# One transformer layer with packed feed-forward weights: the first gate weights prepared one stage earlier, down pieces and row sums spread over other units

## The reference

```python
x = x + _layernorm(attention(_layernorm(x), Wq, Wkv, Wo, bo))
x = x + _layernorm(ffn(_layernorm(x), gate_Wq, up_Wq, down_Wq, scales, zeros))

# attention: 32 query heads of 32, 8 groups of keys and values, causal softmax
# ffn:
Wg, Wu, Wd = dequantize(gate), dequantize(up), dequantize(down)   # (w4 - zero) * scale, groups of 64
g = einsum('bsh,ih->bsi', x, Wg)
u = einsum('bsh,ih->bsi', x, Wu)
h = silu(g) * u
return einsum('bsi,hi->bsh', h, Wd)
```

## Time and profile before

| | us |
|---|---|
| median of 3 runs (2747.84 to 2748.58) | 2748.23 |
| profiled execution | 2746.93 |
| its span | 2745.1 |
| PE busy | 2628.1 |
| DVE busy | 1608.5 |
| POOL busy | 1164.5 |
| ACT busy | 953.3 |
| SP and ACT issue DMAs; moved in all | 209.93 MB |

### The profile page before, as it was taken

The page is one execution under the profiler, slowest core; times in us unless marked ns, Lnnn a source line. Parts: engine busy times, 40 slices in busy tenths (PEclk is TensorE's granted clock), DMA queues, the critical chain, the costliest instruction groups (busy, mean ns, idle before and its releaser), DMA issues. The chain is left out here.

```text
span 2745.1 us, 42051 instructions
## 1 busy us (share of the span) xinstructions
PE 2628.1 (96%) x17032; PEld 1113.8 (41%) x17032; DVE 1608.5 (59%) x1993; ACT 953.3 (35%) x1676; POOL 1164.5 (42%) x641
## 2 busy tenths in 40 slices
PE   6999899999999999999987999999999997999998
PEld 3445533333333333324443444444444443444443
DVE  6331778777787787825677688777777770101001
ACT  3111266666666666671112222332232220000000
POOL 0000177777777777771222334555555550100001
PEclk9999999999999999999998999999999998999999
DMA  4223101011010110003223322333333347332220
GB/s 172 81 77 97 31 17 30 17 46 30 17 30 17 43 33 17 2 1 128 94 76 106 94 74 92 107 111 101 113 109 105 106 143 264 113 120 72 72 72 31
DMA packets 180351, 209.93 MB, mean 76 GB/s; under 512 B 17620, under 2 KB 138708, under 8 KB 180180
## 3 DMA queue, kind: packets, MB, share of 16 engines
q1 hardware_dynamic: 175440, 198.11, 22.3%
q10 hardware_dynamic: 4740, 9.44, 0.9%
HBM read 146.28 MB, written 61.08 MB: 76 GB/s over the span
## 5 line engine op out<-in xcount | busy, mean ns | idle before, releaser
L788 POOL TENSOR_TENSOR c_prob<-c_prob 128x1024 f32<-128x1024 f32 (+1 forms) x285 | 600.2, 2125 | 517.7 <-ACT c_prob L651 515.3
L670 DVE TENSOR_REDUCE c_maxes<-c_s 128x2 f32<-128x1024 f32 (+3 forms) x640 | 645.6, 1058 | 198.8 <-PE c_s L500 198.8
L651 ACT ACTIVATE c_prob<-c_s 128x512 f32<-128x512 f32 (+1 forms) x1152 | 598.0, 571 | 300.3 <-PE c_s L522 185.0
L522 PE MATMUL c_s<-c_q,c_k 97*128 97x512 f16 (+3 forms) x1280 | 367.5, 353 | 10.1 <-ACT c_prob L651 1.7
L1346 PE MATMUL e_ps<-x_hi,e_w_hi 128*128 128x512 f16 x832 | 316.1, 380 | 15.4 <-DVE e_w_lo L1419 15.4
L1347 PE MATMUL e_ps<-x_lo,e_w_hi 128*128 128x512 f16 x832 | 316.0, 380 | 0.0
L1348 PE MATMUL e_ps<-x_hi,e_w_lo 128*128 128x512 f16 x832 | 315.9, 380 | 0.0
L537 PE MATMUL c_ctx<-c_prob,v_sb 128*32 128x512 f32 (+3 forms) x2560 | 293.7, 540 | 0.2 <-ACT c_c L635 0.2
L1731 POOL TENSOR_TENSOR e_w<-e_w,e_scales 128x1024 f32<-128x1024 f32 (+2 forms) x67 | 161.3, 2408 | 260.4 <-DVE e_w L1403 260.4
L522 PEld LDWEIGHTS c_s<-c_q,c_k 97*128 97x128 f16 x1280 | 111.4, 97 | 345.9 <-ACT c_prob L651 299.3
L77 DVE BATCH_NORM_STATS2 f_norm_stats<-f_yp 128x6 f32<-128x512 f32 x16 | 11.2, 699 | 409.0 <-PE f_yp L1884 409.0
(11 more groups left out here) (193 smaller groups left out, 3796.3 us busy)
## 6 DMA issues: line engine op xcount, KB each, us to landing
h_hi<-e_hh SPq DMA_DIRECT2D x84, 128.0 KB, 1.8
h_lo<-e_hl SPq DMA_DIRECT2D x84, 128.0 KB, 1.8
b_x<-L_attn_x SPq DMA_DIRECT2D x16, 512.0 KB, 6.3
c_q<-qk_hi SPq DMA_DIRECT2D x64, 128.0 KB, 3.1
d_x<-L_attn_x SPq DMA_DIRECT2D x16, 512.0 KB, 5.2
x_dram<-d_x SPq DMA_DIRECT2D x16, 512.0 KB, 2.6
f_x<-x_dram SPq DMA_DIRECT2D x8, 1024.0 KB, 7.0
out<-f_z SPq DMA_DIRECT2D x8, 1024.0 KB, 5.0
```

Of the source, the lines that this page charges most:

```text
L522: last = nc.tensor.matmul(S2[:, h % 2, at:at + w], K[:, g % 2, k * P:(k + 1) * P], Q[:, g % 2, b, h, q:q + w], start=True, stop=not diag)
L651: nc.scalar.activation(prob(g, s, 0, w)[:, h, :], S2[:, h % 2, 0:w], ACT.Exp, scale=exp_scale).then_inc(exp_done, 1)
L670: last = nc.vector.tensor_reduce(MAXES[:, g % 2, t // TPB, heads, t % TPB, u], S1[:, heads, at:at + w], AX.X, ALU.max)
L788: return nc.gpsimd.tensor_tensor(one, one, two, ALU.add)
```

## The change

Three things, and what they need:

- **First gate weights.** A new class `Opening` owns the buffers for preparing weights that `gate_and_up` made itself before. They lie in the memory of `c_hi` and `c_lo`, which now stay allocated to the end. In `project_context` SP loads the words, zeros and scales of the first two gate chunks once TensorE has read the context for the last time, ahead of the last `store_rows`. VectorE unpacks chunk 0 in the last pair's `body`, ahead of the second norm; GpSimd scales it after its last residual sum; ScalarE makes the high half ahead of the last `cut_turned`, VectorE the low half (`trail`) ahead of the same. `gate_and_up` starts with chunk 1.
- **Down pieces.** One piece in (q, 0) for all q except 5, the last included; two more in (1,1), one more in (2,1). The last unit (21,1) has none, (21,0) has one. Pieces from number 2 on are thereby made earlier: 2 and 3 in (1,1), 4 in (2,0), 5 in (2,1), 6 in (3,0), 7 in (4,0). In units of `made_beside` SP stores the piece ahead of the h of that unit.
- **Row sums.** Group (1,0) goes beside the remainder, unit (2,0); (1,1) and (1,2) are in (3,0), and (1,3) alone in (3,1).

In stage 4 the down weights of 16 chunks lie where the context was and those of the last chunk and the rest in a small buffer, so the last part is loaded by three DMAs for each half in place of two.

```diff
@@ -858,6 +861,10 @@
             with sp.Fori(0, PAIRS - 1) as i:
                 store_rows(i)
                 load_rows(i + 1)
+            sp.wait_ge(y_product, 2 * PAIRS)
+            for chunk in range(2):
+                opening.load(sp, chunk)
             store_rows(PAIRS - 1)
             for s in range(2):
                 sp.wait_ge(x1_stored[s], 16 * PAIRS)
@@ -922,6 +929,9 @@
                 if not last:
                     dve.wait_ge(x1_done, 2 * i + 1)
                     read_product(i + 1, 0)
+                else:
+                    dve.wait_ge(y_product, 2 * PAIRS)
+                    opening.unpack(dve)
                 x_norm.on_vector(dve, i, lambda s: dve.wait_ge(x1_done, 2 * i + s + 1), lambda s: X1[:, s, :],
                                  lambda s: XN[:, s, :].rearrange("p (two j q r) -> p two j q r", two=2, r=RUNS, q=P // RUNS),
                                  norm_done,
@@ -936,6 +946,7 @@
             with dve.Fori(1, PAIRS - 1) as i:
                 body(i)
             body(PAIRS - 1, last=True)
+            opening.trail(dve)
             cut_turned(PAIRS - 1)
         @block.scalar
@@ -954,6 +965,7 @@
                 y_norm.on_scalar(act, i)
                 cut_turned(i - 1)
                 x_norm.on_scalar(act, i)
+            opening.lead(act)
             cut_turned(PAIRS - 1)
...
@@ -968,9 +980,10 @@
             residual(0, True)
             with pool.Fori(1, PAIRS) as i:
                 residual(i, False)
-
-
-def gate_and_up(nc, x2_hi, x2_lo, quantised, wd_hi, wd_lo, h_hi, h_lo, first, sem):
+            opening.scale(pool)
+def gate_and_up(nc, x2_hi, x2_lo, quantised, wd_hi, wd_lo, h_hi, h_lo, opening, first, sem):
...
@@ -1026,8 +1037,10 @@
         if q + 1 < PAIRS and p < len(tasks_of(q + 1)):
             task_no[q + 1, p] = len(tasks)
             put(u, (q + 1, p) + tasks_of(q + 1)[p])
-        places = [1] if p == 0 and q + 1 < PAIRS and q != PLAIN else [0, 1] if q + 1 == PAIRS else []
-        for place in places:
+        for place in {0: [1] if q != PLAIN else [],
+                      1: [0, 1] if q + 1 < PAIRS and role(q + 1) == "rest" else [0] if role(q) == "rest" else []}[p]:
             number = sum(1 for t in tasks if t[2] == DOWN)
             if number < len(downs):
                 down_in.setdefault(u, []).append(number)
@@ -1146,13 +1159,12 @@
-    made_beside = {(0, 0): [(0, 0)], (0, 1): [(0, 1)], (1, 0): [(0, 2)], (1, 1): [(0, 3)], (2, 0): [], (2, 1): [],
-                   (3, 0): [(1, 0), (1, 1)], (3, 1): [(1, 2), (1, 3)]}
+    made_beside = {(0, 0): [(0, 0)], (0, 1): [(0, 1)], (1, 0): [(0, 2)], (1, 1): [(0, 3)], (2, 0): [(1, 0)], (2, 1): [],
+                   (3, 0): [(1, 1), (1, 2)], (3, 1): [(1, 3)]}
     T_MADE = 3 * 2 * JC
-    raw_loaded = [sem(f"e_raw_loaded{s}") for s in range(2)]
-    unpacked, shifted, scaled, summed = (sem(f"e_{n}") for n in ("unpacked", "shifted", "scaled", "summed"))
-    cut_hi, cut_lo = sem("e_cut_hi"), sem("e_cut_lo")
+    raw_loaded, unpacked, shifted, scaled = opening.raw_loaded, opening.unpacked, opening.shifted, opening.scaled
+    cut_hi, cut_lo, summed = opening.cut_hi, opening.cut_lo, sem("e_summed")
     down_hi, down_lo, down_hi_stored, down_lo_stored = (
...
@@ -1290,7 +1299,7 @@
                     sp.dma_start(dram[c * P:c * P + n * planes, cols].rearrange("(c p) d -> p c d", c=planes),
                                  buf[0:n, 0:planes, :]).then_inc(stored, 16)
-            for k in range(AT_START + 2):
+            for k in range(AT_START, AT_START + 2):
                 load(k)
             for u in units:
                 for k in beside.get(u, []):
@@ -1313,11 +1322,12 @@
                         for of in range(2):
                             sp.dma_start(first.rows(i, of), h[0:FIRST * P, of * 2 * P:(of + 1) * 2 * P]
                                          .rearrange("(c p) t -> p c t", p=P)).then_inc(first.loaded, 16)
-                if role(q) != "up":
+                downs_first = role(q) != "up" or u in made_beside
+                if downs_first:
                     for number in down_in.get(u, []):
                         store_down(number)
                 for name in hs(q):
-                    if role(q) == "up" and name == hs(q)[2]:
+                    if not downs_first and name == hs(q)[2]:
                         for number in down_in.get(u, []):
                             store_down(number)
                     i = h_no[u + (name,)] - 1
@@ -1395,7 +1405,9 @@
                 last.then_inc(unpacked, 1)
                 if k >= AT_START:
-                    dve.wait_ge(cut_lo, cut_no[unit_of[k][0], weight_cuts(unit_of[k][0])[-1]])
+                    of, beside_p = unit_of[k]
+                    dve.wait_ge(cut_lo, cut_no[of + 1, "W1"] if kind == DOWN and beside_p and i == 0 else
+                                cut_no[of, weight_cuts(of)[-1]])
                 earlier = [t[3] for t in tasks[:k] if t[2] == DOWN and t[1] == i]
                 if earlier:
                     dve.wait_ge(down_lo, earlier[-1] + 1)
@@ -1579,9 +1591,9 @@
                 if role(q) == "both":
                     gated(u, "22")
-            for k in range(AT_START):
+            for k in range(1, AT_START):
                 unpack(k)
-            for name in weight_cuts(0):
+            for name in weight_cuts(0)[1:]:
                 cut(0, name)
             for u in units:
                 for k in beside.get(u, []):
...
@@ -1758,7 +1770,7 @@
                 nc.gpsimd.tensor_tensor(HL[0:n, i % 2, :], H[0:n, i % 2, :], HH[0:n, i % 2, :], ALU.subtract
                                         ).then_inc(lo_done, 1)
-            for k in range(AT_START):
+            for k in range(1, AT_START):
                 scale(k)
             for u in units:
...
+class Opening:
+    def __init__(self, nc, sem, gate, c_hi, c_lo):
+        self.nc, self.gate = nc, gate
+        self.raw_loaded = [sem(f"e_raw_loaded{s}") for s in range(2)]
+        self.unpacked, self.shifted, self.scaled, self.cut_hi, self.cut_lo = (
+            sem(f"e_{n}") for n in ("unpacked", "shifted", "scaled", "cut_hi", "cut_lo"))
+        at = [0, 0]
+        def part(of, dims, dtype):
+            size = 2 if dtype == F16 else 4
+            n = math.prod(dims) * size // 2
+            flat = (c_hi, c_lo)[of][:].rearrange("p k t -> p (k t)")[:, at[of]:at[of] + n]
+            at[of] += n
+            names = "abcd"[:len(dims)]
+            return (flat if dtype == F16 else flat.bitcast(dtype)).rearrange(
+                f"p ({' '.join(names)}) -> p {' '.join(names)}", **dict(zip(names, dims)))
+        self.w_hi, self.w_lo = part(0, (2, 7, BANK), F16), part(0, (2, 7, BANK), F16)
+        self.nibbles = part(0, (2, BANK), I32)
+        self.w, self.raw = part(1, (2, 2, BANK), F32), part(1, (2, BANK), I32)
+        self.zeros, self.scales = part(1, (2, BANK), F32), part(1, (2, BANK), F32)
+        self.s, self.sums = part(1, (3, BANK), F32), part(1, (3, BANK), F32)
+    def load(self, sp, chunk):
+        words, scales, zeros = self.gate
+        run = P // RUNS
+        sp.dma_start(self.raw[:, chunk, :].rearrange("p (j i) -> p j i", j=RUNS),
+                     words.rearrange("(j p) i -> p j i", p=P)[:, :, chunk * P:(chunk + 1) * P]
+                     ).then_inc(self.raw_loaded[chunk], 16)
+        for table, dst in ((zeros, self.zeros), (scales, self.scales)):
+            sp.dma_start(dst[:, chunk, :], table[:, chunk * BANK:(chunk + 1) * BANK].unsqueeze(0)
+                         .broadcast_to([run, RUNS, BANK])).then_inc(self.raw_loaded[chunk], 16)
+    def unpack(self, dve):
+        nc = self.nc
+        dve.wait_ge(self.raw_loaded[0], 48)
+        nc.vector.tensor_scalar(self.nibbles[:, 0, :], self.raw[:, 0, :], 4, 15, ALU.logical_shift_right, ALU.bitwise_and)
+        nc.vector.tensor_scalar(self.nibbles[:, 1, :], self.raw[:, 0, :], 15, None, ALU.bitwise_and
+                                ).then_inc(self.unpacked, 1)
+        dve.wait_ge(self.unpacked, 1)
+        nc.vector.tensor_tensor(self.w[:, 0], self.nibbles[:], self.zeros[:, 0, :].unsqueeze(1).broadcast_to([P, 2, BANK]),
+                                ALU.subtract).then_inc(self.shifted, 1)
+    def scale(self, pool):
+        pool.wait_ge(self.shifted, 1)
+        self.nc.gpsimd.tensor_tensor(self.w[:, 0], self.w[:, 0], self.scales[:, 0, :].unsqueeze(1)
+                                     .broadcast_to([P, 2, BANK]), ALU.mult).then_inc(self.scaled, 1)
+    def lead(self, act):
+        act.wait_ge(self.scaled, 1)
+        self.nc.scalar.activation(self.w_hi[:, 0, 0:2, :], self.w[:, 0], ACT.Copy, scale=GS).then_inc(self.cut_hi, 1)
+    def trail(self, dve):
+        dve.wait_ge(self.cut_hi, 1)
+        self.nc.vector.scalar_tensor_tensor(self.w_lo[:, 0, 0:2, :], self.w[:, 0], GS, self.w_hi[:, 0, 0:2, :],
+                                            ALU.mult, ALU.subtract).then_inc(self.cut_lo, 1)
 class First:
...
```

(16 more changed lines are left out.)

33 lines of the change are left out of this document (17 added, 16 removed).

## The result

| | before | after |
|---|---|---|
| median, 7 runs each | 2747.84 (2745.95 to 2751.88) | 2737.43 (2733.51 to 2739.23) |
| profiled execution | 2746.93 | 2737.43 |
| its span | 2745.1 | 2735.7 |

The ratio is 0.996, 95% interval 0.995 to 0.997; the forecast was 2737.7. Positions are compared inside a trace where it matters, since whole stages move from one execution to the next: the last context product ends at 1424.29 before and 1424.58 after, and anywhere from 1420.74 to 1425.59 in the other traces here, though nothing that was edited runs ahead of it.

What follows compares the result with a forecast made beforehand. TensorE, busy 96% of the span, was taken as the bound, so only its idle time could change. 2746.9 - 9.6 - 11.7 + 10.8 = 2736.4, or 2737.7 us against the median; range 2723 to 2745, likeliest case 2732 to 2742.

Steps and rivals of the forecast that it cites:

- Opening: Start of the gate stage: TensorE's first matmul at 1446.7 instead of 1456.3, 9.6 us gained, bounds 7.5 and 11.8.
- the first nibble operation blocked behind GpSimd's sum: Projection stage's end: VectorE's first nibble operation takes about 2.5 us beside GpSimd's residual sum; rows come 3.0 us later.
- The 15.4 becomes about 6: Sign at the start of the gate stage: TensorE's 15.4 us wait shrinks to about 6.
- next to no idle time from (2,0) to (4,0): Sign in the gate stage: VectorE is almost fully busy from unit (2,0) to unit (4,0).
- Middle: Gate stage: moved downs and sums make the third product of (5,0) start 10.8 us later; bounds -2.4 and +18.
- 0 to 1, I take 0: Unit (1,1): two small downs and a store wait fall into idle time; VectorE 0 to 1 us late, taken as 0.
- End: Before the down stage: without downs in the last unit TensorE starts at 2269.1, 11.7 us gained, bounds 10 and 12.5.
- the early loads: Down-stage loads, said to be next late: issued near 2251, landing about 2263, covered by 6 us.
- VectorE's backlog fits into its idle time: Rival for the gate stage: backlog is taken up before pair 4, no cost there; 2726.9 us, chance 0.25.
- the smaller (3,1) gives nothing back: Rival for unit (3,1): other blocks replace the removed group, 18 us lost; 2745 us, chance 0.12.
- The stacking in pairs 5 and 6: Rival, slower than before: TensorE waits in each fast unit and lateness stacks up; 2755.7 us, chance 0.04.
- The end did shorten: Denies the rival before the down stage that late early loads or last stores prevent shortening; 2749.4 us, chance 0.04.

## Why the prediction was right

- **Opening, forecast -9.6, measured -9.42 (-9.71 inside the traces).** Rows 3.0 us late: 3.1, or 2.8 inside the traces. From the rows to the first matmul 0.5: 0.62. The reason was half wrong. I had the first nibble operation blocked behind GpSimd's sum (2.5 us); both took 0.42, and it was the subtract that stood, 3.24 in place of 1.2 us. It ends 1.1 us after GpSimd's sum. The three together come out nearly the same, since whichever is blocked can go on only once GpSimd's sum is done; that the figure held although another operation stood is luck in part. The nibble operations cost something else: GpSimd's two sums took 5.77 us, before 5.14, and 5.77 too in both kernels with the subtract moved away from them. The Trainium skill ("SBUF — State Buffer", "Who interferes with whom") also says that an instruction of VectorE with two inputs in SBUF contends with one of GpSimd that reads SBUF; the subtract is that, and the 3.24 us agree. The same section of the Trainium skill says that issue order decides who blocks. Both shifts of the subtract agree: each moved the stall elsewhere, to operations that took 2.22 us in place of 0.17 and 4.78 in place of 2.73 beside the scaling.
- **"The 15.4 becomes about 6" was wrong**: it is 2.94. The bracket counts from the last turn, and that moved too: 15.44 - 9.42 - 3.08 = 2.94. The term of the sum did not use it. Another sign was wrong too: VectorE was to have next to no idle time from (2,0) to (4,0), but in (2,1) it is busy 10.69 of 15.63 us. Most of the rest is the wait for scaling and copy that the forecast's own sum for (2,1) held (3.32 us ahead of the cut at 1567.25).
- **Middle, forecast +10.8, measured +12.06.** By the starts of VectorE's units against the start of the stage: up to (2,0) 0.6, forecast 0; (2,0) 10.7, forecast 10.3; (2,1) 5.3, forecast 5.3; (3,0) 2.7, forecast 2.5; (3,1) -7.3, forecast -7.3. Together 12.0. The terms that were mis-sized are the "0 to 1, I take 0" of (1,1), which came out at 0.6, and (2,0), 0.4 too small. The waits of TensorE ahead of P7 follow from these starts; they are not further terms. The new waits were 1.74 us (forecast 0.7) and 8.74 (forecast 9), in the units named.
- **End, forecast -11.7, measured -12.08.** The next thing late would be the early loads: issued from 2253.40 and up to 8.0 us from issue to landing, they are there by about 2264, some 8 us ahead of the down stage (the core moves 318 GB/s from 2263 to 2264 and 11 in the next microsecond). From the start of the down stage to the end of the span it is 464.0 us, before 464.3, so the third DMA of a half and the later loads cost nothing.
- **The rivals.** That VectorE's backlog fits into its idle time (2726.9) failed in (2,0) and (2,1), which grew by 16 us together. That the smaller (3,1) gives nothing back failed by its 12.43 us. The stacking in pairs 5 and 6 did not come: behind P7 the one wait up to the down stage is the 0.21 us at 1727.65. The end did shorten.
- **How near the total is, is partly luck.** The terms missed by +0.2, -0.4 and +1.3 us, 1.1 in all, so they give -9.4 and not -10.5. The medians differ by 10.4, 0.9 more than the profiled executions, and the kernel before ran at a median of 2747.84, 0.4 under the one the forecast was set on. Runs of the kernel after spread over 5.7 us; 0.3 us between forecast and median is not a measure of the forecast.

## What to carry over

Where one engine works through a queue in order and its chain ends in one wait of the bound engine, cost a moved piece of work by how much later each stretch of that queue starts: the terms so read from the trace of after add to 12.0 of 12.06 us, and when the sums or the piece were taken out of the remainder's units, 5.5 and 5.3 us came back, together 10.8. Put moved work into a stretch that has idle time not already a wait for another engine. (21,0) had it; pair 1 took the sums for 0.9 us but asked 3.0 us for a full piece; the remainder's units did not have it. Ask of a wait whether another of the same chain follows it: a slow clock behind the last one was paid in full. An operation taken out from beside another engine's may just set free what blocks the next one.
